# A GNN kernel's src-ordered stage: VectorE copies the m1 slices behind its comparisons, in GpSimd's place

## The reference, cut to what matters

```python
msg_1 = x @ W_m1.T + b_m1                     # per node, 96 wide
msg_2 = x @ W_m2.T + b_m2
msg_e = edge_attr @ W_me.T + b_me             # per edge
msg = relu(msg_1[row] + msg_2[col] + msg_e)   # row = src, col = dst
msg = relu(msg @ W_net.T + b_net)
agg = segment_max(msg, row, num_segments=N_NODES)
out = x @ W_o1.T + b_o1 + (agg @ W_o2.T + b_o2)
```

## Time and profile before

| | |
|---|---|
| runs | 2833.95, 2836.42, 2842.11 us; median 2836.42 |
| profiled execution, span | 2838.6 us |
| src-ordered stage, first load to last scan | 1205 to 1696 us of the span |
| busy over the whole span | PE 2320.7 us (82%), PEld 2014.7 (71%), DVE 2036.0 (72%), ACT 1000.7 (35%), POOL 1860.7 (66%) |
| mean granted TensorE clock | 0.969 |

### The profile page before, as it was taken

One profiled execution on the slowest core, in us unless ns is written; L12 is line 12 of the kernel. 1 busy time (PEld: TensorE's weight loads), 2 busy tenths in 40 slices (PEclk: granted clock), 3 DMA queues, 4 the chain that ended last, 5 costly groups with the idle time before them and its releaser, 6 DMA issues. The chain is left out here.

```text
span 2838.6 us, 89638 instructions
## 1 busy us (share of the span) xinstructions
PE 2320.7 (82%) x22430; PEld 2014.7 (71%) x22431; DVE 2036.0 (72%) x9631; ACT 1000.7 (35%) x2286; POOL 1860.7 (66%) x2595
## 2 busy tenths in 40 slices
PE   7778888888888888799999988876677777777777
PEld 6578777777777777477777766766677666777777
DVE  8678777777777777777787877566666666666666
ACT  7334333333333333144444447222222222222225
POOL 1047777777777777654444437677777777777774
PEclk9789999999999999899999998899999999999999
DMA  5021111111111111188888973222222222222221
GB/s 187 29 57 47 45 45 45 45 45 45 45 45 45 45 45 48 35 218 228 226 226 225 227 194 78 54 54 54 54 54 54 53 54 54 54 55 54 55 53 46
DMA packets 582003, 236.10 MB, mean 83 GB/s; under 512 B 512256, under 2 KB 553772, under 8 KB 581676
## 3 DMA queue, kind: packets, MB, share of 16 engines
q1 hardware_dynamic: 298020, 98.53, 15.3%
q0 software_dynamic: 52736, 93.92, 11.6%
q10 hardware_dynamic: 231176, 42.79, 7.5%
HBM read 142.39 MB, written 98.65 MB: 85 GB/s over the span
## 5 line engine op out<-in xcount | busy, mean ns | idle before, releaser
L1041 POOL DMA_INDIRECT edge_in_src_order<-u,place x784 | 756.6, 965 | 259.9 <-issue 185.2
L1714 POOL DMA_INDIRECT a_rows<-src_table,idx x782 | 742.2, 949 | 248.8 <-issue 237.9
L1791 PE MATMUL ps_h<-a_rows,ident 128*128 x1664 | 237.8, 286 | 247.3 <-SPq L1723 185.4
L1791 PEld LDWEIGHTS ps_h<-a_rows,ident 128*128 128x128 f32 x1664 | 202.6, 192 | 278.9 <-issue 278.7
L1411 POOL COPY m_s<-m 128x144 f32 x832 | 234.0, 325 | 244.0 <-PE ps_pre L1458 242.9
L1831 ACT ACTIVATE h<-ps_h 128x512 f32<-128x512 f32 x208 | 124.2, 597 | 743.6 <-PE ps_h L1796 653.9
L1760 DVE TENSOR_SCALAR ohd_f<-iota_b,dloc_c 128x128 f32<-128x128 bf16 x832 | 199.1, 312 | 209.8 <-PE ps_s L1805 204.1
L1434 DVE TENSOR_TENSOR_SCAN top<-same,top,ps_net 96x512 f32<-96x512 bf16 x207 | 264.1, 1276 | 97.9 <-PE ps_net L1465 97.6
L1335 ACT COPY u<-ps_u 128x384 f32<-128x384 f32 x196 | 93.7, 478 | 604.1 <-DMA edge_in_src_order<-u,place 581.7
L1258 PE MATMUL ps_u<-we_s,attrT 128*128 128x384 f32 x392 | 173.8, 525 | 158.9 <-ACT u L1335 158.9
L1748 DVE TENSOR_TENSOR hsumT<-hsumT,ps_s 128x128 f32 x832 | 238.2, 286 | 84.4 <-DVE deg L1750 1.8
(11 more groups left out here) (357 smaller groups left out, 5400.8 us busy)
## 6 DMA issues: line engine op xcount, KB each, us to landing
u_in<-edge_in_src_order SPq DMA_DIRECT2D x208, 192.0 KB, 3.4
running_max<-row ACTq DMA_DIRECT2D x208, 192.0 KB, 4.2
rowt<-src_row SPq DMA_DIRECT2D x208, 130.0 KB, 3.7
key_b<-edge_keys ACTq DMA_DIRECT2D x832, 1.5 KB
edge_in_src_order<-u,place POOLq DMA_INDIRECT x784, 2.2
a_rows<-src_table,idx POOLq DMA_INDIRECT x782
edge_attributes<-in_edge_attr SPq DMA_DIRECT2D x8, 784.0 KB, 12.0
attr_in<-edge_attributes SPq DMA_DIRECT2D x196, 32.0 KB, 1.9
```

The lines of the kernel that those rows point to most:

```text
L1041: pool.indirect_dma_start(u_d, bass.IndirectOffsetOnAxis(place[:, u, j:j + 1], 0), ur[:, u, j, :], None).then_inc(sent[u], 16)
L1714: pool.indirect_dma_start(a_rows[:, 4 * u + j, :], None, a_d, bass.IndirectOffsetOnAxis(idx[:, u % 4, j:j + 1], 0)).then_inc(got[u % 4], 16)
L1791: m.matmul(ps_h[k][:, j, :], ident[:], a_rows[:].rearrange("p c d -> p (c d)")[:, bass.ds(slot[j], D)], start=(j == 0), stop=False, skip_g ...
```

## The change

GpSimd loses its `stage` function, its semaphore count `passed_pool` and its wait for `one_set`; what is left to it in this block is the memset of the row of ones. VectorE gets `stage` with the same waits, offsets and copies, called after `onehot` at each turn. TensorE's, ScalarE's and SyncE's programs are the same, and so are all tiles and all other semaphores.

```diff
-                passed_pool = sem(t, "passed_pool")
@@ block.gpsimd
                         nc.gpsimd.memset(msg[F:F + 1].rearrange("f u e -> f (u e)"), 1.0).then_inc(one_set, 1)
 
-                        def stage(i, u, n):
-
-                            wait(pool, pre_ready, i - 3)
-                            pass_waits(pool, passed_pool)
-                            at = offsets(nc, mybir.EngineType.Pool, sf_row[0:1, bass.ds(4 * i, 4)], (NB - 1) * 3 * F // 2)
-                            for j in range(4):
-                                last = nc.gpsimd.tensor_copy(m1_s[:, u, j, :], m1[:].bitcast(F32)[:, bass.ds(at[j], 3 * F // 2)])
-                            last.then_inc(m1_ready, 1)
-                        pool.wait_ge(one_set, 1)
-                        pipeline(pool, G, [(0, stage)])
@@ block.vector, behind onehot
+                        def stage(i, u, n):
+                            wait(dve, pre_ready, i - 3)
+                            at = offsets(nc, mybir.EngineType.DVE, sf_row[0:1, bass.ds(4 * i, 4)], (NB - 1) * 3 * F // 2)
+                            for j in range(4):
+                                last = v.tensor_copy(m1_s[:, u, j, :], m1[:].bitcast(F32)[:, bass.ds(at[j], 3 * F // 2)])
+                            last.then_inc(m1_ready, 1)
@@ block.vector, behind scan
-                        pipeline(dve, G, [(4, scan), (0, onehot)])
+                        pipeline(dve, G, [(4, scan), (0, onehot), (0, stage)])
```

## The result

The changed kernel takes 2910.17 us (median of four runs, 2909.74 to 2911.12) against 2835.18 us for the kernel before (median of four, 2832.48 to 2842.11): ratio 1.0256, with an interval of 1.0241 to 1.0272. It is 75 us slower; 2915 was forecast. The profiled executions are 2909.4 and 2838.6 us long, 70.8 apart; single runs of the kernel before differ by up to 10 us, so the two differences agree.

What follows compares the result with a forecast made beforehand. TensorE was taken to bound the kernel at 2.33 us per step; VectorE's 2.72 us over 204 turns adds 79.6 us, less some 2 at the end, net +78 on 2836.4: 2915 us, range 2885 to 2960.

Steps and rivals of the forecast that it cites:

- What bounds the kernel before: Src-ordered stage: TensorE sets the pace at 2.33 us per step; GpSimd's copies are hidden, removing them is worth 0.
- The sequencer's sum, 2.72 us: VectorE's step: register load, address steps, copy issue, next scan's waits and branch add up to 2.72 us instead of 2.33.
- branch step: VectorE's loop branch, once in four steps: 0.4 us, a quarter of which is 0.10 us per step.
- The cause, `same` waiting for the scan just issued: VectorE's sequencer: whatever stands behind `same`, register load first, begins only 1.33 us into the step.
- The engine's own step, 2.38 us: VectorE without its sequencer: 1.78 us before plus 0.60 for four copies, 0.05 over TensorE's 2.33.
- Then the sequencer decides: End of VectorE's step: engine done with the fourth copy at 2.49 us, sequencer ready for the next scan at 2.63.
- The end, 2 us back: End of the src-ordered stage: the last four scans find `net` done or nearly so; some 2 us come back.
- The clock: TensorE's granted clock: stays 1.00 with TensorE 86% busy, so nothing was added for it.
- The lasting fall to half speed: Rival: TensorE, idle 0.4 us per step, is granted 1.2 GHz for good; 470 us more; chance 0.01.
- dearer copies: Rival: VectorE's copies at 0.22 us, or dearer register steps besides, give 2940 to 2959 us; chance 0.15.
- The sequencer getting ahead: Rival: load under the scan, wait chain under the copies, only the engine's 2.38 us counts; 2845 us; chance 0.08.
- GpSimd's contention at the stage's start: Rival: GpSimd's copies slow other engines, so removing them gives 2828 us or less; chance 0.02; expected 4 x 0.1 us.

Runs made afterwards that it cites:

- e4: Kernel before, with GpSimd copying only in the first four steps and TensorE waiting for those alone; ratio 1.0007, 2.328 us per step.
- e6: Changed kernel with VectorE's loop unrolled by eight and eight buffers for `same`, so its wait is four steps older; ratio 1.0003, 2.346 us per step.
- e5: Changed kernel with VectorE's loop unrolled by eight instead of four, buffers as they were; ratio 1.0167, 2.571 us per step.
- e7: Changed kernel with the copy step called between scan and onehot instead of behind onehot; ratio 1.0010, 2.346 us per step.
- e2: Changed kernel with copies read from constant places, so without register load and address steps; ratio 1.0011, 2.347 us per step.
- e9: Changed kernel with each of the four copies 72 words wide instead of 144; ratio 1.0256, 2.697 us per step.
- e11: Changed kernel with the register load split in two of two values each, both used, in the same place; ratio 1.0808, 3.828 us per step.
- e12: Changed kernel with the load split in two of two values, both used, and the copy step between scan and onehot; ratio 1.0192, 2.685 us per step.
- e3: Kernel before with an unused register load added on VectorE behind onehot, which wasn't executed; ratio 0.9996.
- e1: Changed kernel with the copy step between scan and onehot, run on a chip slower in other blocks; ratio 1.0010, step 2.346 us.

## Why the prediction was right, point by point

- **What bounds the kernel before**: TensorE's columns, with GpSimd's copies hidden. e4 shows it: 2.328 us without the copies.
- **The sequencer's sum, 2.72 us**: measured 2.693, term by term: load at 1.42, measured 1.43; first copy at 1.89, measured 1.91; next scan at 2.63, measured 2.59; branch step 0.40 longer, measured 2.99 - 2.59 = 0.40. The small excess lies behind the last copy's issue: the scan's register steps begin at 2.28 instead of 2.30 and take 0.31 us, where I put 0.33 (and my own terms, three of 0.09 and one of 0.07, add up to 0.34). It makes 204 x (2.72 - 2.693) = 5.5 of the 7 us between the 78 us forecast and the 71 of the traces.
- **The cause, `same` waiting for the scan just issued**: shown by e6 against e5, where that wait alone is changed, and by e7, where the load is moved ahead of it. That it is the load with its address steps that the wait holds up is shown by e2; the two were not taken apart.
- **The engine's own step, 2.38 us**: measured 2.346 in e2, e6 and e7. A copy of 144 words has 0.144 us of room (0.15 forecast), and the scan up to 0.01 us less than before.
- **"Then the sequencer decides"**: shown by e9, where shorter copies change nothing.
- **The end, 2 us back**: 7.35 - 5.50 = 1.85 us. The sum against the windows: 204 x (2.693 - 2.329) = 74.3, less 1.9, is 72.4, against 71 in the windows and 70.8 in the spans; the rest, some 1.5 us, stays open (at the stage's start I had put 0, at most 1).
- **The clock**: 0.99 over the stage in both kernels, as the windows at the beginning show, and 1.00 from 1225 to 1750 us of the changed kernel (first line below), with TensorE busy for 493 of these 525 us by its records; no term was needed. The lasting fall to half speed did not come.
- **What I had wrong**: I said that TensorE would idle before `pre` L1458, released by VectorE's copies. It idles before `net`, released by the scan (25.0 us in 400, in the rows above). `net(i - 3)` comes first in TensorE's turn and needs `scan(i - 5)`, which is issued in the same turn of VectorE as `stage(i - 1)`; while TensorE does `net`, `turn` and the turning of the edge rows, the copies catch up, and `pre` never waits. It doesn't change the time, but the forecast of who waits was wrong. In e11, where the copies come 1.2 us later still, `pre` does wait for them.
- **The rivals**: dearer copies are excluded by the measured 0.144 us. The sequencer getting ahead gives 2.346 us, as e6 shows, but not with this wait in this place. GpSimd's contention at the stage's start is gone as expected, and worth nothing that can be measured: `same` takes 0.416 us in the first four steps, where it took 0.511.

```profile
1225.00:1750.00 525.00, 493.45 (x4307) 358.93 (x4305) 493.34 (x1365) 209.25 (x391) 0.00 (x0) 1.00 0.77 196
...
L1414 DVE TENSOR_TENSOR same<-rowt x4: 415/416/416, 1208.2 to 1212.4; 96x512 bf16<-96x512 bf16 x4
```

## What to carry to other kernels

When a step moves to another engine, add up that engine's sequencer as well as its datapath: register loads, address steps, waits and the loop's branch run in order, and behind a wait for the operation just issued only the work issued after the wait can hide them. Here that was `same`, which covered the load of 0.345 us; the address step, the next scan's register steps and the branch stood open. Put work that begins with a register load ahead of such a wait (e7), or make the wait older with more buffers (e6, there with fewer branches as well); here either ends at 2.346 us, which wins back 0.35 of the 0.36 us per step that the change had lost. And before freeing an engine, ask who waits for it: GpSimd's copies held up nobody, so the best version on VectorE is within 0.1% of the kernel before and none is faster.

## What the runs showed of the hardware that was not expected

- A register load of two values on VectorE took 0.52 us at least, and up to 0.98 in e11 and 1.07 in e12, against a median of 0.345 and a least of 0.340 for loads of four in the changed kernel (single ones longer, up to 0.65); open why.
- On two of the chips used, the three blocks with the indirect DMAs are much slower (in e3 by some 435, 55 and 490 us from their first to their last instruction, all others by no more than 3), with a lower granted clock of TensorE, while the src-ordered stage is untouched. The windows of e3, whose program is in effect the kernel before, and then those of the kernel before on the first chip (columns as at the beginning):

```profile
200.00:1150.00 950.00, 689.70 (x6531) 578.08 (x6530) 506.06 (x3406) 268.01 (x654) 507.97 (x525) 0.82 0.13 32
1700.00:2100.00 400.00, 400.00 (x3784) 304.96 (x3783) 318.93 (x515) 183.69 (x344) 192.11 (x688) 1.00 0.88 226
```

```profile
200.00:1150.00 950.00, 793.88 (x9474) 699.12 (x9471) 731.68 (x4933) 363.67 (x950) 721.57 (x751) 1.00 0.18 46
1300.00:1600.00 300.00, 300.00 (x2838) 228.65 (x2837) 239.45 (x387) 138.03 (x258) 144.47 (x516) 1.00 0.89 226
```

In 950 us that chip gets through 6531 matmuls instead of 9474 at a clock of 0.82 instead of 1.00. Whether the clock or the DMAs come first there was not tried. The src-ordered stage is the same on either: e1 there and e7 here both have 2.346 to 2.347 us per step.
